# A fused chain of four layers on one Trainium2 core: the first loads and the first pair of sequences put in another order

## What is computed

```python
x = x + (einsum('bsi,bio->bso', x, W0[id]) + b0[id])          # 16 experts, one for each sequence
x = x + (x @ W1.T + s[a] * ((x @ A[a].T) @ B[a].T))           # one matrix, 8 adapters of rank 16
x = x + attention(x, Wq, Wk, Wv, Wo, paged keys and values)   # window of 256, RMS norm, rotation
x = x + (einsum('bct,bcd->bdt', x, W3[subject]) + b3)         # 8 subjects
```

## Time and profile before

| | |
|---|---|
| median of 3 runs (lowest to highest) | 953.3 us (952.72 to 953.48) |
| span of the profiled execution, first to last instruction | 948.6 us |
| TensorE busy | 907.5 us, 96% |
| VectorE, GpSimd, ScalarE busy | 651.1, 522.3, 444.3 us |
| DMA | 218.51 MB, 230 GB/s on average |

### The profile page before, as it was taken

The page is one execution under the profiler, slowest core; times in us unless marked ns, Lnnn a source line. Parts: engine busy times, 40 slices in busy tenths (PEclk is TensorE's granted clock), DMA queues, the critical chain, the costliest instruction groups (busy, mean ns, idle before and its releaser), DMA issues.

```text
span 948.6 us, 23332 instructions
## 1 busy us (share of the span) xinstructions
PE 907.5 (96%) x6477; PEld 660.8 (70%) x6477; DVE 651.1 (69%) x1853; ACT 444.3 (47%) x1190; POOL 522.3 (55%) x502
## 2 busy tenths in 40 slices
PE   5789999999999999999997899999999999999997
PEld 3456666766666667666676777877777887787785
DVE  5345545667768774556754678777878877888875
ACT  2333333333333333333322566666666666666663
POOL 2136455464564657855556666566565665656530
PEclk9799999999999999999998799999999999999999
DMA  9978988778788787887844566666666676567741
GB/s 295 265 230 282 330 308 290 252 261 289 247 282 276 244 291 255 271 295 247 284 159 152 183 188 203 199 210 186 198 197 212 200 225 203 181 209 212 221 135 46
DMA packets 100413, 218.51 MB, mean 230 GB/s; under 512 B 30187, under 2 KB 36168, under 8 KB 92178
## 3 DMA queue, kind: packets, MB, share of 16 engines
q1 hardware_dynamic: 66290, 145.27, 47.0%
q0 software_dynamic: 25088, 57.74, 20.5%
q10 hardware_dynamic: 8992, 15.00, 4.9%
HBM read 210.39 MB, written 33.86 MB: 257 GB/s over the span
## 4 chain that ended last, share of the span: by engine, by line
PE 51%; POOL 18%; issue 15%; DMA 7%; SPq 4%; DVE 2%; ACT 1%; ACTq 1%; POOLq 0%; DVEq 0%
PE banks L823 9%; PE banks L775 9%; PE banks L811 7%; PE banks L798 6%; POOL rms L471 5%; DMA ring<-in_rope 5%; PE banks L752 4%; PE banks L859 3%; POOL ring L475 3%; POOL x_in L461 3%; PE banks L816 3%; POOL q_rot L480 2%; PE banks L753 1%; PE banks L791 1%; POOL ring L482 1%
## 5 line engine op out<-in xcount | busy, mean ns | idle before, releaser
L561 POOL DMA_INDIRECT ring<-new_rows,idx x128 | 129.4, 1011 | 82.5 <-PE banks L775 40.3
L471 POOL TENSOR_TENSOR rms<-ss,neg_half 128x12 f32<-128x12 f32 x31 | 70.8, 2284 | 185.4 <-DVE ss L1259 185.4
L992 ACT ACTIVATE big<-big,neg_max 128x320 f32<-128x320 f32 x256 | 141.4, 554 | 3.1 <-DVE neg_max L1317 2.7
L1317 DVE CUSTOM_DVE_ANT_0 big<-banks,mask 128x320 f32<-128x320 f32 x256 | 114.6, 486 | 27.4 <-PE banks L775 26.0
L602 PE MATMUL banks<-ring 128*64 128x512 f32 x512 | 117.8, 601 | 0.9 <-DMA ring<-in_w 0.9
L982 ACT ACTIVATE kt<-banks 128x384 f32<-128x384 f32 x128 | 61.8, 483 | 97.5 <-PE banks L753 97.5
L775 PE MATMUL banks<-kt,q_in 64*128 64x128 f32 (+2 forms) x768 | 88.6, 364 | 1.3 <-ACT kt L982 1.3
L550 POOL DMA_INDIRECT ring<-new_rows,idx x64 | 61.7, 965 | 47.0 <-PE banks L798 42.7
L1354 DVE TENSOR_SCALAR big<-big,recip 128x320 f32<-128x320 f32 x256 | 85.5, 396 | 2.3
L775 PEld LDWEIGHTS banks<-kt,q_in 64*128 64x128 f32 x768 | 74.4, 189 | 14.4 <-issue 8.4
L811 PEld LDWEIGHTS banks<-pt,ring 128*64 128x64 f32 x1024 | 55.4, 136 | 38.1 <-DVE pt L1299 25.4
(11 more groups left out here) (177 smaller groups left out, 1989.0 us busy)
## 6 DMA issues: line engine op xcount, KB each, us to landing
ring<-in_w SPq DMA_DIRECT2D x62, 1024.0 KB, 7.5
ring<-in_xt SPq DMA_DIRECT2D x32, 256.0 KB, 2.7
x_in<-in_x SPq DMA_DIRECT2D x32, 256.0 KB, 5.8
bias_in<-in_b SPq DMA_DIRECT2D x64, 128.0 KB, 6.4
x_dram<-x SPq DMA_DIRECT2D x32, 256.0 KB, 6.9
q_dram<-q_t ACTq DMA_DIRECT2D x32, 256.0 KB, 5.7
new_rows<-kv_out SPq DMA_DIRECT2D x32, 256.0 KB, 6.7
q_in<-q_dram SPq DMA_DIRECT2D x32, 256.0 KB, 2.7
```

Of the source, the lines that this page charges most:

```text
L471: nc.gpsimd.tensor_tensor(rms[:, s, :], ss[:, s, :], neg_half[:, :], ALU.pow).then_inc(rms_ready, 1)
L561: pool.indirect_dma_start(out=kv[:, s, c, :], out_offset=None, in_=new_rows, in_offset=bass.IndirectOffsetOnAxis(ap=idx[:, b, 1 + c:2 + c] ...
L992: nc.scalar.activation(prob[:, s % 2, PLACE[g] * NK:(PLACE[g] + 1) * NK], sm[:, s % 2, g, :], ACT.Exp, bias=neg_max[:, s % 2, g:g + 1], sc ...
L1317: V.tensor_tensor_reduce(sm[:, s % 2, g, :], ps_s[g], mask[:, s % 2, k0:k0 + NK], 1.0, 3.0e38, ALU.add, ALU.min, accum_out=neg_max[:, s % ...
```

## The change

What it does:
- SyncE issues identity and `lora_a` first, in front of its wait for the numbers. W1 comes in two halves with a semaphore each. The B rows of pair 0 are loaded by SyncE (`load_adapters`) behind W1, those of pair 1 behind `load_first`, so ahead of `load_in(1, ...)`. ScalarE no longer issues these four loads.
- ScalarE and VectorE make the parts of W1 half by half. The adapter copies of pair 1 move behind the high part of Wq. The high part of Wk and Wv and the adapters of pair 2 move into pair 1, behind the high part of x2.
- VectorE does x2 of pair 0 ahead of the low part of Wq. The six steps on `first_key`, `odd` and `beyond` move into `take_tables`.
- TensorE in pair 0: high W1 with high x1, then `adapt_down`, then the two groups with low parts. In pair 1: all three groups for the queries, and after them all three for keys and values.

The diff, cut to its core:

```diff
             sp.dma_start(xt[:, 0, :, :], a["xt"][0]).then_inc(ld_xt[0], 16)
+            sp.dma_start(ident[:, :], a["ident"]).then_inc(ld_ident, 16)
+            sp.dma_start(lora_a[:, :, :], a["la"]).then_inc(ld_la, 16)
             sp.wait_ge(ld_ids, 16)
...
-                sp.dma_start(ident[:, :], a["ident"]).then_inc(ld_ident, 16)
-                sp.dma_start(w1_stage, a["w1"]).then_inc(ld_w1, 16)
-                sp.dma_start(lora_a[:, :, :], a["la"]).then_inc(ld_la, 16)
+                for i, c in enumerate(W1_PARTS):
+                    sp.dma_start(w1_stage[:, c, :], a["w1"][:, c, :]).then_inc(ld_w1[i], 16)
+                load_adapters(0)
                 sp.dma_start(wqkv_stage[:, :, 0:D], a["wq"]).then_inc(ld_wq, 16)
...
+            def load_adapters(k):
+
+                if k == 0:
+                    sp.wait_ge(pb_set, 1)
+                for h in range(2):
+                    n = sp.value_load(ids_sb[0:1, 3, k * 2 + h:k * 2 + h + 1], min_val=0, max_val=NA - 1)
+                    sp.dma_start(pair_b[T * h:T * h + ROLE_ROWS, k, :], a["lb"][bass.ds(n, 1)].rearrange("o q d -> (o q) d")).then_inc(
+                        ld_pb[k], 16)
+
             load_first()
+            load_adapters(1)
             load_in(1, 0, 1)
...
-                        pe.wait_ge(w_hi_ready, 2)
+                        pe.wait_ge(w_hi_ready, 3)
                     for ps_out, n0 in ((ps_q, 0), (ps_kv, D)):
                         if isinstance(k, int) and k == 1 and n0 == D:
-                            pe.wait_ge(w_hi_ready, 3)
+                            continue
...
                         if isinstance(k, int) and k == 1 and n0 == D:
+                            pe.wait_ge(w_hi_ready, 4)
+                            for c in range(DC):
+                                nc.tensor.matmul(ps_out[:, :], x2t_hi[:, c, :], wqkv_hi[:, c, n0:n0 + D], start=(c == 0), stop=False)
                             pe.wait_ge(wqkv_lo_ready, 2)
...
-                    if isinstance(k, int) and k < 2:
+                    if isinstance(k, int) and k == 1:
                         adapt_down(k, s)
                     wait(pe, x2_ready, k)
+                    pe.wait_ge(x1hi_ready, k + 1)
                     if isinstance(k, int) and k == 0:
-                        pe.wait_ge(w_hi_ready, 1)
-                        pe.wait_ge(w1_lo_ready, 1)
-                    pe.wait_ge(x1hi_ready, k + 1)
-                    pe.wait_ge(x1lo_ready, k + 1)
+                        pe.wait_ge(w_hi_ready, 2)
+                    else:
+                        pe.wait_ge(x1lo_ready, k + 1)
                     for x_part, w_part in ((x1t_hi, w1_hi), (x1t_hi, w1_lo), (x1t_lo, w1_hi)):
+                        if isinstance(k, int) and k == 0 and w_part is w1_lo:
+                            adapt_down(0, s)
+                            pe.wait_ge(w1_lo_ready, 2)
+                        if isinstance(k, int) and k == 0 and x_part is x1t_lo:
+                            pe.wait_ge(x1lo_ready, 1)
...
-            act.wait_ge(ld_w1, 16)
-            nc.scalar.activation(w1_hi[:, :, :], w1_stage, ACT.Copy).then_inc(w_hi_ready, 1)
+            for i, c in enumerate(W1_PARTS):
+                act.wait_ge(ld_w1[i], 16)
+                nc.scalar.activation(w1_hi[:, c, :], w1_stage[:, c, :], ACT.Copy).then_inc(w_hi_ready, 1)
...
-            for k in range(2):
-                take_adapters(k, k, copy=False)
...
+                if isinstance(k, int) and k == 1:
+                    act.wait_ge(ld_wkv, 2 * 16)
+                    nc.scalar.activation(wqkv_hi[:, :, D:], wqkv_stage[:, :, D:], ACT.Copy).then_inc(w_hi_ready, 1)
+                    take_adapters(2, 0)
...
-                    for n in range(2):
-                        take_adapters(n, n, load=False)
+                    take_adapters(0, 0, load=False)
                     round_adapters(0, 0, 0)
...
                     nc.scalar.activation(wqkv_hi[:, :, 0:D], wqkv_stage[:, :, 0:D], ACT.Copy).then_inc(w_hi_ready, 1)
-                if isinstance(k, int) and k == 0:
-                    act.wait_ge(ld_wkv, 2 * 16)
-                    nc.scalar.activation(wqkv_hi[:, :, D:], wqkv_stage[:, :, D:], ACT.Copy).then_inc(w_hi_ready, 1)
+                    take_adapters(1, 1, load=False)
...
-                if on(k, -2, NP):
+                if on(k, -2, NP) and not (isinstance(k, int) and k == 0):
                     take_adapters(k + 2, s)
...
+            def first_keys():
...
             def take_tables():
 
+                first_keys()
...
-                    dve.wait_ge(w_hi_ready, 1)
-                    V.tensor_tensor(w1_lo[:, :, :], w1_stage, w1_hi[:, :, :].bitcast(F32), ALU.subtract).then_inc(w1_lo_ready, 1)
+                    for i, c in enumerate(W1_PARTS):
+                        dve.wait_ge(w_hi_ready, 1 + i)
+                        V.tensor_tensor(w1_lo[:, c, :], w1_stage[:, c, :], w1_hi[:, c, :].bitcast(F32), ALU.subtract).then_inc(w1_lo_ready, 1)
...
                     split_adapters(k + 1, r)
-                if isinstance(k, int) and k == 0:
-                    split_inputs(0)
...
                     V.tensor_tensor(x2[:, s, :], ps_l1[:, :], x1[:, s, :], ALU.add).then_inc(x2_ready, 1)
+                if isinstance(k, int) and k == 0:
+                    split_inputs(0)
```

More of the change, by code:

```diff
@@ L186, in build @@
         ps_last, ps_mix = ps[0:2], ps[2:4]
-        ld_ids, ld_small, ld_ident, ld_la, ld_w1, ld_wq, ld_wkv, ld_late, ld_wo = (sem(n) for n in (
-            "ld_ids", "ld_small", "ld_ident", "ld_la", "ld_w1", "ld_wq", "ld_wkv", "ld_late", "ld_wo"))
+        ld_ids, ld_small, ld_ident, ld_la, ld_wq, ld_wkv, ld_late, ld_wo = (sem(n) for n in (
+            "ld_ids", "ld_small", "ld_ident", "ld_la", "ld_wq", "ld_wkv", "ld_late", "ld_wo"))
+        ld_w1 = [sem(f"ld_w1{i}") for i in range(2)]
         cols_i, win_idx_ready, win_loaded = sem("cols_i"), sem("win_idx_ready"), sem("win_loaded")
@@ L247, in loop @@
                 step(n, n // slots, n % slots)
+        W1_PARTS = (slice(0, DC // 2), slice(DC // 2, DC))
         COLUMN_PARTS, WHOLE = ((0, D // 2), (D // 2, D)), ((0, D),)
@@ L870, in _, with take_adapters @@
             act.dma_start(reals[:, :], a["reals"]).then_inc(ld_small, 16)
-            act.wait_ge(ld_w1, 16)
-            nc.scalar.activation(w1_hi[:, :, :], w1_stage, ACT.Copy).then_inc(w_hi_ready, 1)
-            def take_adapters(k, s, load=True, copy=True):
+            for i, c in enumerate(W1_PARTS):
+                act.wait_ge(ld_w1[i], 16)
+                nc.scalar.activation(w1_hi[:, c, :], w1_stage[:, c, :], ACT.Copy).then_inc(w_hi_ready, 1)
+            def take_adapters(k, s, load=True):
                 for h in range(2):
@@ L880, in take_adapters @@
                             ld_pb[s], 16)
-                    if copy:
-                        last = nc.scalar.activation(
-                            pair_a[:, s, h, :, 0:ROLE_ROWS].rearrange("p c (q r) -> p c q r", r=RANK),
-                            lora_a[:, :, bass.ds(n * RANK, RANK)].unsqueeze(2).to_broadcast([P, DC, ROLES, RANK]), ACT.Copy,
-                            scale=scaling[:, bass.ds(n, 1)])
-                if copy:
-                    last.then_inc(pa_ready, 1)
+                    last = nc.scalar.activation(
+                        pair_a[:, s, h, :, 0:ROLE_ROWS].rearrange("p c (q r) -> p c q r", r=RANK),
+                        lora_a[:, :, bass.ds(n * RANK, RANK)].unsqueeze(2).to_broadcast([P, DC, ROLES, RANK]), ACT.Copy,
+                        scale=scaling[:, bass.ds(n, 1)])
+                last.then_inc(pa_ready, 1)
             def round_adapters(k, j, s):
@@ L1073, in _ @@
                 link(V.tensor_scalar(xa_parts[T * h:T * h + T, T - T * h:P - T * h], mrow[T * h:T * h + T, 0:T], 0.0, None, ALU.mult))
-            link(V.tensor_scalar(first_key[:, :], kvl_row[:, :], -1.0, float(WIN), ALU.mult, ALU.add))
-            link(V.tensor_scalar(first_key[:, :], first_key[:, :], fcols[:, TCOL:TCOL + 1], None, ALU.max))
-            link(V.tensor_scalar(odd_i[:, :], kvl_row[:, :], 1, None, ALU.bitwise_and))
-            link(V.tensor_scalar(odd[:, :], odd_i[:, :], 1.0, None, ALU.mult))
-            link(V.tensor_tensor(first_key[:, :], first_key[:, :], odd[:, :], ALU.subtract))
-            link(V.tensor_scalar(beyond[:, :], odd[:, :], BIG, None, ALU.mult))
             link(V.tensor_scalar(gain_in[:, :, :], gain_in[:, :, :], 1.0, None, ALU.add))
@@ L1084, in _ @@
             V.tensor_copy(scol[:, 4:5], scol[:, 3:4]).then_inc(gains_ready, 1)
+            def first_keys():
+                link(V.tensor_scalar(first_key[:, :], kvl_row[:, :], -1.0, float(WIN), ALU.mult, ALU.add))
+                link(V.tensor_scalar(first_key[:, :], first_key[:, :], fcols[:, TCOL:TCOL + 1], None, ALU.max))
+                link(V.tensor_scalar(odd_i[:, :], kvl_row[:, :], 1, None, ALU.bitwise_and))
+                link(V.tensor_scalar(odd[:, :], odd_i[:, :], 1.0, None, ALU.mult))
```

(3 more changed lines are left out.)

4 lines of the change are left out of this document (2 added, 2 removed).

## The result

| | before | changed | ratio |
|---|---|---|---|
| median of 8 runs each, us | 953.6 (952.4 to 958.27) | 945.27 (943.19 to 951.12) | 0.992, 95% interval 0.9895 to 0.9944 |
| span of the profiled execution, us | 948.6 | 942.2 | |
| first experts matmul of pair 1, us | 44.49 | 39.49 | |

A forecast was written before the change was run, and what follows sets the result against it. TensorE bounds the kernel except at the start, set by L plus the work behind it. Savings of 3.2 us behind L and 2.0 at L gave 5.2: span 948.6 to 943.4, plus 4.7 for the median, 948.1 us, range 946.2 to 950.9.

The forecast's parts named there:

- L: Landing of the second pair's adapter rows in the start: 27.3 us, bounds 26.2 and 28.5, 2.0 us ahead of 29.34.
- What bounds the start: The start is set by L plus what VectorE and ScalarE put between L and x2 of pair 0.
- The saving behind L: From L to x2 high in the start: 3.6 us instead of 6.78, so 3.2 us saved.
- rival 1: Start: pair 1's rows land by time since issue, L 28.5 to 30.5, gain 2.0 to 4.0 us; chance 0.14.
- rule of the turns between queues: Adapter loads lose their passing of long loads when moved to SyncE's queue; by this alone L would be 33.5.
- The 24 matmuls: TensorE behind x2 high in the start: again 7.7 us, waiting for nothing new; clock may move the sum by 1 us.
- Pair 0: Pair 0's edits lie beside L: x1 moves −0.5 to +0.5 us, slack 2.1 to 4.4 us, worth and cost nothing.
- The six steps in pair 2: Six small VectorE steps, 1.4 us, moved to pair 2 make a correction some 0.2 us late and cost nothing.
- The shift is kept: From pair 1's experts through the loop the start's gain counts in full; margins 2.3 and 2.1 us.
- rival 2: Start: lower clock ends sooner or L is 26.2; gain 6.5 to 8 us, time 945.3 to 946.8; chance 0.10.
- the range: Whole kernel's time: 946.2 to 950.9 us, reaching over half of rival 1 and rival 2.

The follow-up runs named there:

- before, fills at pair 2 and the last: Kernel before plus matmuls of no result: 18 `warm_up` calls at pair 2, 19 and 6 transposes of the identity at the last pair; 952.66 us, ratio 1.0005.
- loads alone: Kernel before with only the four adapter-row loads moved from ScalarE's queue to SyncE's, at their places in the changed kernel; 951.14 us, ratio 0.9973.
- order alone: Changed kernel with the loads of the kernel before: adapter rows on ScalarE's queue, identity and adapter matrix at their old places; 948.99 us, ratio 0.9955.
- changed, second: The changed kernel measured again without an edit; 948.11 us, ratio 0.9945 to the kernel before.
- changed, third: The changed kernel measured once more without an edit; 947.02 us, ratio 0.9946 to the kernel before.
- start fill: Changed kernel plus 36 and 6 transposes of the identity on TensorE ahead of and behind pair 0's transposes of x2; 943.78 us, ratio 0.9916.
- end fill: Changed kernel plus 19 and 6 transposes of the identity on TensorE around the last pair's transposes of x2; 944.78 us, ratio 0.9921.

## Why the prediction was right or wrong

The marks of the profiled executions, all from the traces in order of time (L is the start of the second rounding on ScalarE, E1 the first experts matmul of pair 1):

| kernel | L | E1 | E1 − L | pair 1 to 3 | pair 31 to last |
|---|---|---|---|---|---|
| before | 29.36 | 44.49 | 15.1 | 28.25 | 461.1 |
| before, fills at pair 2 and the last | 29.92 | 45.29 | 15.4 | 30.2 | 459.7 |
| loads alone | 28.02 | 42.89 | 14.9 | 28.5 | 462.6 |
| order alone | 31.70 | 42.82 | 11.1 | 30.3 | 457.7 |
| changed | 27.98 | 39.49 | 11.5 | 28.4 | 459.0 |
| changed, second | 26.86 | 38.46 | 11.6 | 28.4 | 463.0 |
| changed, third | 28.32 | 40.35 | 12.0 | 28.3 | 461.0 |
| start fill | 28.12 | 38.40 | 10.3 | 29.8 | 458.6 |

- **What bounds the start.** Right: L plus what lies behind it. The column E1 − L has two values, 15 with the old order and 11 to 12 with the new, whatever the loads do.
- **The saving behind L.** Said 3.2 us up to x2 high, measured 3.41 (6.78 − 3.37). I had taken ScalarE as the later path, L + 3.6; its two adapter activations took 0.78, not 0.92, and it was VectorE's and TensorE's path that came last, at L + 3.37, with L + 3.35 given for it.
- **L.** Said 27.3 with bounds of 26.2 and 28.5, measured 27.98, 26.86 and 28.32; six other kernels with these loads at these places have 27.66 to 28.34 and once 29.38, beyond the bound. The median of the nine is 28.1, so against 29.36 and 29.92 the loads were worth some 1.5 us, not 2.0. The argument by the place in the queue held; the argument by time since issue (rival 1) did not: SyncE issued the second of the two at 21.85, not 19.4, since its queue was held up longer, and the load landed after 6.1 us. The Trainium skill's rule of the turns between queues ("DMA: Bandwidth & Descriptors", "Queues, rings and completion order") was no obstacle: on a queue of its own each of the four rows needed 6.0 to 8.2 us, on SyncE's 5.3 and 6.1 for pair 1 and 7.8 and 8.4 for pair 0. What it would have given, L at 33.5, did not come.
- **The 24 matmuls.** Said 7.7, measured 7.49 (39.49 − 32.00), with no new wait in the key/value products.
- **Pair 0.** The mechanism (slack) was right, sizes were off: x1 moved by +1.57 us, not by −0.5 to +0.5, since the second halves of pair 0's expert weights let TensorE go on only at 14.31 (12.04 before), and these eight matmuls then took 3.68 instead of 1.94 us at the lower clock. The first matrix was converted at 20.72, not 18.9: its second half came only for 19.66. The sum of pair 0 ended at 25.68, inside the 24.4 to 26.7. E1 does not move with it.
- **The six steps in pair 2.** Nothing, as said: pair 1 to 3 takes 28.3 to 28.4 us in the three profiles of the changed kernel and 28.25 before.
- **The shift is kept.** Right, but for 0.5 to 0.9 us from pair 3 to pair 31 in the three profiles, which I cannot name; against the kernel before, other kernels of the series lie between −0.1 and +1.1 there.

So the sum, 5.2 us, is what the start gave: 5.0 in the first pair of profiles, and 4.1 to 6.8 over all pairs of the two old starts and the three new ones. That the two terms hit the sum so closely is in part luck: the term behind L was 0.2 too small and that of L some 0.5 too large. The number of the first eight runs is rival 2's (945.3 to 946.8), but not by its mechanism: L was not 26.2 and the 24 matmuls did not get shorter. **What failed is the range.** Its step was "a rise sooner or later moves the sum by up to 1 us either way", which looked at the clock in the 24 matmuls of the start alone. In the rest of the kernel, which the range put at nothing, the clock moves more: from pair 31 to the last matmul the three profiles of the changed kernel take 459.0, 463.0 and 461.0 us with the same instructions, and pair 1 to 3 goes from 28.25 to 30.3 over the kernels of the table. The hint stood in front of me: the profiled execution of before lies, by its span, 4.7 us under the median, and I left this "as it is". In all executions with both numbers the time is 1.8 to 2.0 us above the span; so the profiled one of before was some 2.8 us faster than its median, a spread in one kernel that was half of the gain forecast, and medians of a few runs wander by a part of it (945.27, 948.11 and 947.02 for one program). A range of 944.5 to 951 would have held all three. It is not shown that the clock alone put the first of them 2 us under the others.

## What to carry to other kernels

At a start with waits, write the chain as one landing L plus what each engine does in its order behind L, and price order and loads apart: here order was worth 3.4 us behind L in four traces, with L from 26.9 to 31.7, the loads some 1.5 us of L, and the next bound (the weights of pair 1) lay 2 us behind. Before giving a range, compare the profiled span with the runs' median; a difference that is larger than what lies around the span is the kernel's own spread. The mean granted clock of each run, held against its time, tells that spread from the gain of an edit. A hole of TensorE that no edit can close can be filled with matmuls of no result, for some 2 us here over several kernels, if they are counted as they run (18 calls were 36 matmuls) and end before the awaited operand comes; whether the time won is still there some pairs later has to be looked up, and with the start fill it was not.

## What the runs showed of the hardware

- The lower clock behind a hole is not a property of the code alone. In pair 2 a hole of 2.2 us was followed by the upper level in the changed kernel's first profile (eight matmuls 2.09 us) and one of 2.44 us by the lower in the kernel with the end fill (3.05 us), whose program is the same up to there.
- In the first products of phase two, where TensorE has holes of 0.6 to 0.7 us between short groups, the lower level stayed for 10 us in the profile of before, for 13.5 us in the second of the changed kernel (516 to 530 us, clock 0.51) and for 10 us in the third, and in the first it did not fall on these products at all. With the other low stretches behind pair 31 this makes 459.0 to 463.0 us for one program, 4.0 us of 945, more than either the order or the loads gave.
- The time of an execution follows its mean granted clock: of 21 executions of the changed kernel the seven at 0.984 and less took 949.02 us in the median, the seven at 0.989 and more 945.28.
